# Graph attention plus mixture of experts on one core: the skip products of the edge stage are taken out of the query products and come twelve steps later

## The reference

```
q = (xn @ Wq + bq).reshape(n, H, D)        # xn: layer-normed x
k = (xn @ Wk + bk) ...   v = (xn @ Wv + bv) ...
alpha = sum(q[dst] * k[src], -1) / sqrt(D)
m = segment_max(alpha, dst)
ex = exp(alpha - m[dst]);  denom = segment_sum(ex, dst)
out = segment_sum(ex / (denom[dst] + 1e-16) * v[src], dst)
return out + xn @ Wskip + bskip
```

## Time and profile before

| | |
|---|---|
| median of 3 runs | 1462.64 us (1459.58 to 1465.21) |
| the profiled execution, its own time | 1453.31 us |
| its span in the profile | 1451.7 us |
| mean clock that PE was granted | 0.954 |
| PE, DVE, ACT, POOL busy in the span | 1220.1, 1075.5, 800.7, 916.6 us |
| edge stage: first and last `prod` (line 990) | 93.7 and 805.4 us, 232 of them |

### The profile page before, as it was taken

One profiled execution on the slowest core, in us unless ns is written; L12 is line 12 of the kernel. 1 busy time (PEld: TensorE's weight loads), 2 busy tenths in 40 slices (PEclk: granted clock), 3 DMA queues, 4 the chain that ended last, 5 costly groups with the idle time before them and its releaser, 6 DMA issues. The chain is left out here.

```text
span 1451.7 us, 24099 instructions
## 1 busy us (share of the span) xinstructions
PE 1220.1 (84%) x6837; PEld 945.9 (65%) x6837; DVE 1075.5 (74%) x2561; ACT 800.7 (55%) x2506; POOL 916.6 (63%) x875
## 2 busy tenths in 40 slices
PE   7997676677776776767776889999999999999998
PEld 3444454445444454544454568899898899999898
DVE  7747887878777787878787889886876655556555
ACT  1265867575757676666657645665543344444442
POOL 3266666666666666666665447876775577667665
PEclk9999999998989889899889999999999999999999
DMA  7487876666666666767665120111000000000002
GB/s 228 150 253 205 242 205 190 193 200 187 202 182 201 189 201 187 204 187 208 186 194 154 37 72 30 52 30 43 8 15 23 1 23 22 8 15 16 1 12 78
DMA packets 74087, 175.39 MB, mean 121 GB/s; under 512 B 11516, under 2 KB 36667, under 8 KB 73961
## 3 DMA queue, kind: packets, MB, share of 16 engines
q0 software_dynamic: 37632, 124.28, 30.7%
q1 hardware_dynamic: 34657, 48.25, 10.0%
q10 hardware_dynamic: 1672, 1.33, 0.3%
HBM read 159.91 MB, written 13.91 MB: 120 GB/s over the span
## 5 line engine op out<-in xcount | busy, mean ns | idle before, releaser
L696 POOL DMA_INDIRECT ring<-kv_rows,k_srcI x464 | 459.5, 990 | 274.4 <-issue 124.3
L763 ACT ACTIVATE ring<-ring 128x64 f32<-128x64 f32 x1800 | 438.6, 336 | 10.9 <-issue 9.9
L1319 POOL TENSOR_TENSOR wm<-k_gf,wm 128x512 fp32r<-128x512 f32 (+2 forms) x224 | 259.1, 1161 | 140.8 <-DVE wm L1828 140.8
L1422 ACT ACTIVATE k_gf<-psF,k_scT 128x512 f32<-128x512 f32 (+2 forms) x224 | 161.8, 724 | 250.5 <-PE psF L1597 247.2
L815 PE MATMUL psA<-ring,oh 128*128 128x260 f32 x912 | 268.9, 422 | 10.3 <-DVE k_acc L1024 8.3
L783 PE MATMUL psQ<-k_q,ohT 128*128 x1392 | 218.9, 297 | 68.3 <-issue 59.8
L1828 DVE CAST wm<-k_gf 128x512 fp32r<-128x512 f32 (+2 forms) x224 | 161.2, 727 | 151.4 <-ACT k_gf L1422 151.2
L990 DVE TENSOR_TENSOR prod<-psQ,ring 128x512 f32<-128x512 f32 x232 | 157.6, 679 | 88.8 <-remote 34.0
L783 PEld LDWEIGHTS psQ<-k_q,ohT 128*128 128x128 bf16 x1392 | 127.5, 103 | 124.0 <-issue 95.1
L815 PEld LDWEIGHTS psA<-ring,oh 128*128 128x128 f32 x912 | 174.5, 213 | 37.5 <-issue 10.1
L1030 DVE TENSOR_REDUCE alpha<-prod 128x8 f32<-128x512 f32 x232 | 155.7, 671 | 0.2
(11 more groups left out here) (289 smaller groups left out, 2634.2 us busy)
## 6 DMA issues: line engine op xcount, KB each, us to landing
ohT<-step_destinations SPq DMA_DIRECT2D x29, 512.0 KB
ring<-kv_rows,k_srcI POOLq DMA_INDIRECT x464
kv_rows<-kvst SPq DMA_DIRECT2D x25, 260.0 KB, 2.6
we<-in_L_ffn_W SPq DMA_DIRECT2D x16, 256.0 KB, 2.8
residual<-qst SPq DMA_DIRECT2D x25, 128.0 KB
xs<-in_x SPq DMA_DIRECT2D x2, 1024.0 KB, 8.9
resin<-residual SPq DMA_DIRECT2D x4, 512.0 KB
we<-in_L_ffn_Wo SPq DMA_DIRECT2D x8, 256.0 KB, 2.8
```

Of the source, the lines that this page charges most:

```text
L696: nc.gpsimd.indirect_dma_start(out=ring[:, LT * (j % CP) + k, j // CP:j // CP + 2, :].rearrange("p t e -> p (t e)"), out_offset=None, in_= ...
L763: last = nc.scalar.activation(row[:, 0:D], row[:, 0:D], ACT.Copy, scale=row[:, D:HW_])
L1319: nc.gpsimd.tensor_tensor(low[:, i % 2, m, 0:w], gf[:, n % 4, 0:w], high[:, i % 2, m, 0:w], ALU.subtract).then_inc(s_gl, 1)
L1422: nc.scalar.activation(gf[:, n % 4, 0:cols(g)], ps, ACT.Relu, bias=bias, scale=scale).then_inc(s_ev, 1)
```

## The change

The query product of a block and its skip product become two products of 256 columns each. The query products stay where they were. The skip product of block t is made by `skip(t)` on PE in step t + 12, into a bank of its own, `psS`; this bank is free because the chain of maxima now has all its small results in `psM`. ACT rounds the query to bf16 right from PSUM (`high`), DVE subtracts from PSUM too (`remainder` into a new tile `qrem`), and `middle` comes one block later. ACT copies the skip product to `skst` and zeroes `acc` in `skip_out(t)`, in step t + 13; SP stores from there. Since `acc` is zeroed later, the additions wait for the zeroing of a block each. The fetches of `ohT` on SP are put between the stores by their step.

```diff
+SKIP = 12
...
-            for t in range(QEARLY + CP):
+            for t in range(NB):
+                if t + SKIP + 1 >= 2 * CP and (t + SKIP + 1) % CP == 0 or t == 0:
+                    cc = max(2, (t + SKIP + 1) // CP + 1)
+                    fetch(cc, cc % 2, False)
                 store(t)
-            fetch(2, 0, False)
-            for t in range(QEARLY + CP, NB):
-                store(t)
-            fetch(3, 1, False)
...
-            def project_out(t):
-
+            def high(t):
                 act.wait_ge(s_qp, t + 1)
+                nc.scalar.activation(q3[:, 0, t, :], query(t), ACT.Copy).then_inc(s_qhi, 1)
+
+            def middle(t):
+                act.wait_ge(s_qr1, t + 1)
+                nc.scalar.activation(q3[:, 1, t, :], qrem[:, t % 2, :], ACT.Copy).then_inc(s_qmid, 1)
+
+            def skip_out(t):
+
+                act.wait_ge(s_sk, t + 1)
                 if t >= 2:
-                    act.wait_ge(s_qlo, t - 1)
                     act.wait_ge(s_reso[t % 2], 16 * (t // 2))
-                nc.scalar.activation(qst[:, t % 2, :], psA[t % NA][:, :], ACT.Copy).then_inc(s_qres, 1)
-                act.wait_ge(s_qres, t + 1)
-                nc.scalar.activation(q3[:, 0, t, :], qst[:, t % 2, 0:HID], ACT.Copy).then_inc(s_qhi, 1)
+                nc.scalar.activation(skst[:, t % 2, :], psS[:, 0:HID], ACT.Copy).then_inc(s_skout, 1)
                 nc.scalar.activation(acc[:, t, 0:HID].rearrange("p (k n) -> p k n", k=KC),
                                      iotaF[:, :].unsqueeze(1).broadcast_to([P, KC, P]), ACT.Copy, scale=0.0).then_inc(s_zero, 1)
-                act.wait_ge(s_qr1, t + 1)
-                nc.scalar.activation(q3[:, 1, t, :], qst[:, t % 2, 0:HID], ACT.Copy).then_inc(s_qmid, 1)
...
                 if fresh and QEARLY + j < NB:
-                    project_out(QEARLY + j)
+                    high(QEARLY + j)
+                if fresh and QEARLY + j <= NB:
+                    middle(QEARLY + j - 1)
+                if 0 <= RING * i + j - SKIP - 1 < NB:
+                    skip_out(RING * i + j - SKIP - 1)
...
             def project(t):
 
                 if t >= NA:
-                    pe.wait_ge(s_qres, t - NA + 1)
+                    pe.wait_ge(s_qr1, t - NA + 1)
                 for k in range(KC):
-                    nc.tensor.matmul(psA[t % NA][:, :], acc[:, t, k * P:(k + 1) * P], wqs[:, k, :], start=(k == 0), stop=False)
-                nc.tensor.matmul(psA[t % NA][:, :], onesr[:, :], bqs[:, :], start=False, stop=True).then_inc(s_qp, 1)
+                    nc.tensor.matmul(query(t), acc[:, t, k * P:(k + 1) * P], wqs[:, k, 0:HID], start=(k == 0), stop=False)
+                nc.tensor.matmul(query(t), onesr[:, :], bqs[:, 0:HID], start=False, stop=True).then_inc(s_qp, 1)
+
+            def skip(t):
+
+                if t >= 1:
+                    pe.wait_ge(s_skout, t)
+                for k in range(KC):
+                    nc.tensor.matmul(psS[:, 0:HID], acc[:, t, k * P:(k + 1) * P], wqs[:, k, HID:2 * HID], start=(k == 0), stop=False)
+                nc.tensor.matmul(psS[:, 0:HID], onesr[:, :], bqs[:, HID:2 * HID], start=False, stop=True).then_inc(s_sk, 1)
...
+                if 0 <= RING * i + j - SKIP < NB:
+                    skip(RING * i + j - SKIP)
...
             def remainder(t):
                 dve.wait_ge(s_qhi, t + 1)
-                nc.vector.tensor_tensor(qst[:, t % 2, 0:HID], qst[:, t % 2, 0:HID], q3[:, 0, t, :], ALU.subtract).then_inc(s_qr1, 1)
+                if t >= 2:
+                    dve.wait_ge(s_qlo, t - 1)
+                nc.vector.tensor_tensor(qrem[:, t % 2, :], query(t), q3[:, 0, t, :], ALU.subtract).then_inc(s_qr1, 1)
...
+                    if b < NB:
+                        dve.wait_ge(s_zero, b + 1)
```

More of the change, by code:

```diff
@@ L589, in attend @@
         fac = sb("fac", [BP, H])
-        qst = sb("qst", [BP, 2, 2 * HID])
+        qrem = sb("qrem", [BP, 2, HID])
+        skst = sb("skst", [BP, 2, HID])
         psQ = [pb(f"psQ{b}", [P, 512]) for b in range(NQ)]
@@ L594, in attend @@
         psM = pb("psM", [P, 512])
[L595 to L598, removed]
+        psS = pb("psS", [P, 512])
+        GM, TAILS, CIN, FAC, HEADS, BIN = 264, 328, 396, 400, 404, 472
+        tails = psM[0:1, TAILS:TAILS + H * (W + 1)].rearrange("p (h w) -> p h w", h=H)
+        heads = psM[0:1, HEADS:HEADS + H * (W + 1)].rearrange("p (h w) -> p h w", h=H)
         s_set = sem("s_set")
@@ L623, in walk, with query @@
                 at(place // RING, place % RING, place < RING)
+        def query(t):
+            return psA[t % NA][:, 0:HID]
         def live(i, j, fresh, lag=0):
@@ L653, in store @@
             def store(t):
-                sp.wait_ge(s_qres, t + 1)
-                sp.dma_start(res_v[:, t, :], qst[:, t % 2, HID:2 * HID]).then_inc(s_reso[t % 2], 16)
+                sp.wait_ge(s_skout, t + 1)
+                sp.dma_start(res_v[:, t, :], skst[:, t % 2, :]).then_inc(s_reso[t % 2], 16)
             sp.wait_ge(s_drel, 16)
@@ L676, in _ @@
             sp.dma_start(io["roots"].rearrange("l (q b) -> q l b", b=16), keep["vf"][:, :, :]).then_inc(s_hvd, 16)
-            for cc in range(CR, C):
+            for cc in range((NB - 1 + SKIP + 1) // CP + 2, C):
                 fetch(cc, cc % 2, False)
@@ L829, in rest @@
                     pe.wait_ge(s_mv, NV * m + V_INH)
-                    nc.tensor.matmul(psR[0:R, 128:129], inh[:, :, :].rearrange("p h w -> p (h w)"), one[0:1, 0:1],
+                    nc.tensor.matmul(psM[0:R, CIN:CIN + 1], inh[:, :, :].rearrange("p h w -> p (h w)"), one[0:1, 0:1],
                                      start=True, stop=True).then_inc(s_mp, 1)
@@ L836, in rest @@
                     pe.wait_ge(s_mv, NV * m + V_FD)
-                    nc.tensor.matmul(psR[0:R, 384:385], iv[:, :, :].rearrange("p h w -> p (h w)"), one[0:1, 0:1],
+                    nc.tensor.matmul(psM[0:R, BIN:BIN + 1], iv[:, :, :].rearrange("p h w -> p (h w)"), one[0:1, 0:1],
                                      start=True, stop=True).then_inc(s_mp, 1)
@@ L934, in maximum @@
                     dve.wait_ge(s_mp, mp + T_CARRY)
-                    nc.vector.tensor_copy(cin[:, :], psR[0:R, 128:129]).then_inc(s_mv, 1)
+                    nc.vector.tensor_copy(cin[:, :], psM[0:R, CIN:CIN + 1]).then_inc(s_mv, 1)
                 if at == (3, 1):
@@ L973, in maximum @@
                     at_noh = (j // CP - 1) % CR
-                    nc.vector.tensor_scalar(fac[:, :], psM[0:BP, 400:400 + H], noh[:, at_noh:at_noh + 1], None,
+                    nc.vector.tensor_scalar(fac[:, :], psM[0:BP, FAC:FAC + H], noh[:, at_noh:at_noh + 1], None,
                                             ALU.add).then_inc(s_mv, 1)
@@ L1050, in at @@
                     dve.wait_ge(s_mv, NV * m + V_FAC)
-                    if fresh and j < ADD_LAG:
-                        dve.wait_ge(s_zero, NB)
+                    if br < NB:
+                        dve.wait_ge(s_zero, br + 1)
                     if not (fresh and j < ADD_LAG):
```

16 lines of the change are left out of this document (9 added, 7 removed).

## The result

The changed kernel took 1470.97 us (median of 22 runs, 1462.54 to 1474.93), the kernel before 1465.86 us beside it (22 runs): ratio 1.003, 95% interval 1.0018 to 1.0042. It became slower, by about 5 us, where 8 us less were forecast. By its mechanism rival 1 (the start is held) is nearest, although it expected no loss; by number the 5 us lie between its +2.5 and the +9 of rival 2.

A forecast was written before the change was run, and what follows sets the result against it. No engine was taken as full in the edge stage; waits no program part holds were to stay. Before step 0 -9.2, steps 0 to 16 -6, steps 16 to 37 +6.9: -8.3 us, from 1462.64 to 1454.3 us, range 1445 to 1471.

The forecast's parts named there:

- rival 1: Gathers show only when DMA engines fall idle, holding `prod` of step 0 at 93.5 us; end moves -1.5 to +2.5; chance 0.24.
- rival 2: Skip products wait in `skst` for stores to land, lengthening 25 steps by 0.6 us: +9 us, 1472; chance 0.21.
- I take these waits for something that the program doesn't hold, which stays, and the gathers for prompt: Steps 0 to 16: long waits without a shown releaser, about 9 us, remain, and gathers are not late.
- `prod` of step 0 at 84.4 instead of 93.67: Before step 0: narrower query products and rounding from PSUM let the first `prod` come earlier, -9.2 us, bounds 0 to -11.
- Steps 0 to 16, -6 us: Less PE work and no ACT wait for stores: 46 us instead of 51.9; bounds 48.6 and 41 us.
- Steps 16 to 37, +6.9 us: Moved skip products, copies and zeroing make a step 3.3 us: 69.3 instead of 62.4 us; bounds 0 and +22.
- Behind step 37: Steps after 37: same program at the same pace, an unchanged 3.08 us a step.
- The single costs: A 256-column product on PE costs 1.06 us; `remainder` reading PSUM instead of SBUF costs nothing.
- the queue in lockstep of the forecast: Steps 16 to 37: `skip` waits for ACT's previous copy, the next expansion queues behind it; 0.25 us a step for waits.
- Rival 3: Steps 16 to 37: giving back costs nothing, absorbed by idle time on PE and ACT; -15 us, 1447.5; chance 0.13.
- theory E: From the experiments, not the prediction: TensorE's lower granted clock in the emptier steps 0 to 16 costs; no chance given.

The follow-up runs named there:

- first and third measurement: Two of six timings, each beside the kernel before: the changed kernel took 1.003 of it in the first and 1.0019 in the third.
- credit4: Changed kernel with gathers of four steps in place of eight allowed ahead of the first `prod`: 1468.97 us, 1.0033 of the kernel before.
- before_again: The kernel before, unchanged, measured once more beside itself for a second profile: ratio 1.0009.
- half_gathers: Changed kernel with one gather a step in place of two from step 32 on: 0.9743 of the kernel before.
- after_again: The changed kernel, unchanged, measured once more for a second profile: 0.9952 of the kernel before.
- psum_only: Changed kernel's rounding from PSUM and shared bank alone, products 512 wide, skip half copied in place: 0.9966 of the kernel before, repeats 0.9982 and 0.9976.
- no_skip_work: Changed kernel without the skip products and their copies, stores sending zeros: 0.9954 of the kernel before, repeats 0.9943, 0.9947 and 0.9955.

## Why the prediction was wrong

**The failed step** is "I take these waits for something that the program doesn't hold, which stays, and the gathers for prompt", and the start that hangs on it: "`prod` of step 0 at 84.4 instead of 93.67". The gathers were indeed prompt, as the landing by step 5 had said. But the waits without a releaser were TensorE's signals: by the trace of the kernel before, the updates that the four had waited for stand at 108.85, 121.29, 136.64 and 175.50 us, and the products that make them had ended at 102.77, 118.71, 132.49 and 168.56. On this kind of chip such signals come late with gathers in flight, and a start moved under the sixteen gathers runs into them. -9.2 us became +1.5 and -0.5 (first and third measurement). On prompt chips the step had no such fault: 92.53 became 85.18, and eight profiles there of programs that are the same up to this point have 82.35 to 85.59, 84.3 in the mean. credit4 showed 84.21 on a late one.

**Steps 0 to 16, -6 us**: +1.3 and +0.9 on late chips; -5.9 on a prompt one (44.74 to 38.85). On late chips VectorE and ScalarE still waited for TensorE's signals there, so less work on PE gave nothing. One term was read wrongly, or at least not shown: the 3.31 us of ACT at 105.31 were put down to the store of block 11, but the same copy (block 13) in before_again waited 6.27 us for a signal of TensorE whose product had ended 5.6 us before it ran.

**Steps 16 to 37, +6.9 us**: +5.5 and +1.6 on late chips, inside the bounds. On a prompt one +11.5 (50.38 to 61.85): the pace that comes out, 2.95 us, is nearer to ACT's 3.05 than to the 3.3 taken; but the kernel before does 2.40 there, DVE being all that holds it.

**Behind step 37** nothing was to change. On late chips I can't tell it from the spread of executions. On prompt ones step 37 was 1.8 us earlier (one profile each, and two of half_gathers, the same program up to step 31, differ by 2.7 us there) and step 231 4.8 us: GpSimd's pace decides, not where step 37 stands.

**The single costs were right.** A half on PE took 0.98 to 1.1 us; `remainder` from PSUM took 417 ns against 415 ns of `lowest` from SBUF in the changed kernel. The Trainium skill, page "VectorE: DVE Perf Modes", section on the errata, gives an operand in PSUM 62 cycles more than one in SBUF; this trace does not agree.

**Rivals.** Rival 1 was right on the start and gave the other outcome too kindly: it counted on 141.1 us at step 16, which came at 148.40. Its reason was not the right one, for it is TensorE's signals and not the gathers' that come late. Rival 2 had the sign, not the mechanism: from 146 to 206 us after_again waited 1.7 us in all for stores, and the changed kernel's two profiles on late chips show no wait for one. What they do show is the queue in lockstep of the forecast: PE's weight loads for `psS` waited 5.3 and 4.8 us in all for ACT's copy. Rival 3 (giving back is absorbed) is what prompt chips show, by GpSimd and not by idle time of PE and ACT, and what it leaves is -6.5 us.

In the two late pairs step 37 is 8.3 and 2.1 us later, beside 5.1 and 2.7 us between the medians. That TensorE's late signals took the forecast gain away, at the start and in the steps up to 16, is shown; what made a loss of it isn't. **Open:** which part is due to the moved skip products, as psum_only and no_skip_work met no late chip; what the lower granted clock costs there (0.84 from 94 to 146 us, before 1.00), as theory E was refuted on prompt chips only; why the chips differ; and by what the gathers make a signal late.

## What to carry to other kernels

A wait whose releaser had long ended, and which is put down to nothing in the trace, is a cost with a cause of its own: ask what is in flight whenever it is seen, before work is moved under it, and expect moved work to meet it again. Read who has the full pace behind the changed stretch: where the issuing of gathers sets the end, only its standing time counts. And a result of half a per cent may change sign from one chip to the next; profile both kernels on the chip that times them.

## What the runs showed of the hardware

- The same kernel (before) took 1333 to 1336 us on four chips and 1465 us in two other measurements; the difference is all in the edge stage (steps of 2.5 and 3.1 us), with instructions of equal length: `prod` 677 and 679 ns, a gather 1.00 and 0.99 us.
- On the slower kind 39% of TensorE's kept semaphore updates from 69 to 680 us (864 of 2207 in five profiles) stand more than 1 us behind the modelled end of the product, up to 14.9 us, while TensorE itself went on; 6% of ScalarE's, none of VectorE's. With the DMA engines idle, and in the stage ahead, which gathers nothing, there was no late one. On the faster kind there was none in fifteen profiles, with the same gathers.
- TensorE's granted clock fell to its lower level (0.50 of 2.4 GHz) from 87 to 100 us in the changed kernel on a late chip, while it stood idle from 84.3 to 87.95. In after_again, on a prompt chip, it was 0.93 up to 94 us and 1.00 from there to 146. No experiment showed the clock to decide anything here.
